# First-pass score chunks of 384 columns dealt out by a table, and GpSimd masking two rows at once and taking over subtractions from VectorE

## The reference

```python
q, k, v = xh @ Wq + bq, xh @ Wk + bk, xh @ Wv + bv       # 8 heads of 16 features
p = pe @ Wp
content = einsum('bqhd,bkhd->bhqk', q + u_bias, k)
pos_score = _rel_shift(einsum('bqhd,khd->bhqk', q + v_bias, p))
score = (content + pos_score) / sqrt(e)
attn = softmax(score, axis=-1)                           # needs each row's maximum
x = x + einsum('bhqk,bkhd->bqhd', attn, v).reshape(b, s, e) @ Wo + bo
# router: x @ Wr1, norm, gelu, @ Wr2, softmax, the two best experts of a token
# each expert: (x @ W1[e])[linear half] * gelu(x @ W1[e])[gate half] @ W2[e]
```

## Time and profile before

| | |
|---|---|
| median of 3 runs | 1703.7 us |
| the profiled execution: its own time | 1698.55 us |
| its span | 1696.8 us |
| busy share of the span | PE 91%, PEld 71%, DVE 83%, ACT 66%, POOL 65% |
| mean granted TensorE clock | 0.948 |

### The profile page before, as it was taken

One profiled execution on the slowest core, in us unless ns is written; L12 is line 12 of the kernel. 1 busy time (PEld: TensorE's weight loads), 2 busy tenths in 40 slices (PEclk: granted clock), 3 DMA queues, 4 the chain that ended last, 5 costly groups with the idle time before them and its releaser, 6 DMA issues. The chain is left out here.

```text
span 1696.8 us, 50747 instructions
## 1 busy us (share of the span) xinstructions
PE 1551.2 (91%) x12534; PEld 1207.3 (71%) x12535; DVE 1402.8 (83%) x5272; ACT 1111.8 (66%) x2303; POOL 1105.3 (65%) x2090
## 2 busy tenths in 40 slices
PE   2599999999999999999999999999952699999997
PEld 1367677777677767777767776777741699999997
DVE  3389889989989988998998998799864588888886
ACT  2127776777777777777777777677730577777775
POOL 3337767776776776777677677567673276666666
PEclk8569999999999999999999999899975799999999
DMA  5624634643653463464355346246453243433433
GB/s 162 192 55 137 184 99 114 182 127 103 170 149 97 137 186 101 112 181 128 103 169 149 97 137 184 71 125 172 127 162 126 43 57 55 57 52 55 57 51 49
DMA packets 131859, 199.97 MB, mean 118 GB/s; under 512 B 18392, under 2 KB 93032, under 8 KB 131648
## 3 DMA queue, kind: packets, MB, share of 16 engines
q1 hardware_dynamic: 105792, 177.20, 36.9%
q0 software_dynamic: 25856, 20.27, 7.9%
HBM read 108.24 MB, written 75.33 MB: 108 GB/s over the span
## 5 line engine op out<-in xcount | busy, mean ns | idle before, releaser
L1063 DVE CUSTOM_DVE_ANT_0 junk<-pA,lmask 128x512 bf16<-128x512 f32 x1056 | 687.1, 683 | 67.6 <-PE pA L651 49.1
L965 ACT ACTIVATE prob<-pB 128x512 f32<-128x512 f32 x384 | 229.8, 599 | 200.9 <-PE pB L670 115.1
L1547 POOL DMA_INDIRECT out<-yb,dst x144 | 231.2, 1605 | 134.7 <-ACT yb L1621 82.7
L672 PE MATMUL pB<-QL,K 97*128 97x512 f32 (+3 forms) x768 | 285.2, 371 | 1.4 <-ACT upper_diag L965 1.2
L649 PE MATMUL pA<-K,QL 96*128 96x512 f32 (+3 forms) x792 | 284.0, 360 | 0.8 <-DVE acc L1069 0.4
L670 PE MATMUL pB<-QU,K 97*128 97x512 f32 (+3 forms) x640 | 266.7, 417 | 0.2
L967 ACT ACTIVATE prob<-pB 128x512 f32<-128x512 f32 x384 | 227.9, 593 | 12.4 <-PE pB L672 4.1
L651 PE MATMUL pA<-K,QU 96*128 96x512 f32 (+3 forms) x660 | 232.8, 354 | 1.6 <-DVE acc L1063 0.3
L688 PE MATMUL pC<-prob,vext 128*17 128x256 f32 x3088 | 217.3, 384 | 0.1
L556 POOL TENSOR_TENSOR prob<-prob,upper_diag 128x128 f32<-128x128 f32 x384 | 179.9, 469 | 31.9
L670 PEld LDWEIGHTS pB<-QU,K 97*128 97x128 f32 x640 | 121.6, 190 | 99.3 <-issue 61.7
(11 more groups left out here) (305 smaller groups left out, 3658.5 us busy)
## 6 DMA issues: line engine op xcount, KB each, us to landing
QL<-split_operands SPq DMA_DIRECT2D x67, 256.0 KB
QU<-split_operands SPq DMA_DIRECT2D x67, 256.0 KB
K<-split_operands SPq DMA_DIRECT2D x67, 256.0 KB
xg<-routed_rows SPq DMA_DIRECT2D x76, 132.0 KB
split_operands<-c_h SPq DMA_DIRECT2D x18, 512.0 KB
split_operands<-c_l SPq DMA_DIRECT2D x18, 512.0 KB
QL<-split_operands SPq DMA_DIRECT2D x67, 128.0 KB
QU<-split_operands SPq DMA_DIRECT2D x67, 128.0 KB
```

Of the source, the lines that this page charges most:

```text
L672: mm = pe.matmul(pB[:, q0 + up:q0 + HALF], K[0:r, s, k], QL[0:r, s, q0 + up:q0 + HALF], start=True, stop=True)
L965: act.activation(p[:, 0:HALF], pB[:, 0:HALF], ACT.Exp, scale=SCALE).then_inc(p_exp, 1)
L1063: v.tensor_tensor_reduce(out, src[:, :], lmask[:, at:at + HALF], 1.0, -3.0e38, ALU.add, ALU.max, acc[:, s, qb, n % 2:n % 2 + 1]).then_inc( ...
L1547: po.indirect_dma_start(dram["out"], bass.IndirectOffsetOnAxis(dst[k][:, a:a + 1], 0), yb[k][:, a, :], None, compute_op=ALU.add).then_inc( ...
```

## The change

**First pass.** It has 24 chunks of 384 columns for each head, three for each block of 128 query rows. The 1152 columns of a query block are now the 1024 keys and its own diagonal block once more: chunk columns up to the diagonal take QL, and those behind it take QU with the keys moved back by 128, so that the diagonal block comes in both forms. One mask `smask` serves all. Columns are as many as before (24 x 384 = 16 x 512 + 8 x 128 = 9216). How many chunks each step gets stands in a table `SHARE` of 8 x 9 numbers between 0 and 5; PE does the first before the second half of the second pass, two more behind it, and what is left behind the context.

**GpSimd.** It masks and adds two rows in one instruction each, at u = 2, 4, 6 and 8, on a view of two `prob` tiles that now lie beside each other. It takes from DVE the six subtractions that read SBUF alone and, at u = 3, `dsup` for the next head. The first batch's low halves stay on DVE. Scatters, position products and residual additions on GpSimd move, most of them to odd steps.

**DVE.** Two low halves (`gu_l`) are left, counted by a semaphore of their own, and `maxima` is one instruction. DVE now waits for `dsup` before it writes new super scores.

```diff
+CHUNK = 3 * P
+SPANS = (S + P) // CHUNK
+S1U = NB * SPANS
-        lmask, umask = sb("lmask", [P, 15 * P], BF16), sb("umask", [P, P])
+        smask = sb("smask", [P, 16 * P], BF16)
-        prob = [keep["b2"]] + [sb(f"prob{i}", [P, S]) for i in range(1, RING)]
+        ring = [keep["b2"], sb("prob23", [P, 2, S])]
+        prob = [ring[i // 2][:, i % 2, :] for i in range(RING)]
-        LOW_AT = {(1, 2): 0, (2, 3): 1, (2, 7): 2, (3, 2): 3, (3, 6): 4, (4, 1): 5, (4, 3): 6, (4, 4): 7}
+        LOW_AT = {(3, 6): 4, (4, 4): 7}
+        SPLIT_AT = {(0, 3): 0, (1, 8): 1, (2, 8): 2, (3, 3): 3, (3, 7): 5, (4, 2): 6}
+        DSUP_AT = 3
...
-        ORDER = (0, 1, 2, 3, 4, 5, 6, 7, 16, 8, 9, 10, 17, 11, 12, 13, 14, 15)
+        SHARE = ((5, 1, 3, 3, 3, 4, 1, 3, 1), (4, 1, 2, 2, 3, 5, 2, 4, 1), (2, 2, 3, 2, 3, 3, 3, 2, 4), (0, 3, 2, 2, 4, 3, 3, 3, 4),
+                 (4, 5, 2, 2, 2, 3, 1, 1, 4), (3, 2, 0, 2, 5, 3, 2, 2, 5), (4, 3, 3, 3, 3, 4, 1, 1, 2), (4, 2, 2, 2, 4, 2, 1, 2, 5))
+        def share(h, u):
+            return range(sum(SHARE[h][:u]), sum(SHARE[h][:u + 1]))
         def piece(n):
-            qb, k0 = n // HPB, (n % HPB) * HALF
-            return qb, k0, min(max(P * (qb + 1) - k0, 0), HALF)
+            qb, c = divmod(n, SPANS)
+            return qb, c, min(max(P * (qb + 1) - CHUNK * c, 0), CHUNK)
# GpSimd
+            def low(nb, n):
+                po.wait_ge(hi_done, have)
+                po.tensor_tensor(parts[name][1][:, cut], src, parts[name][0][:, cut].bitcast(F32), ALU.subtract).then_inc(low_done, 1)
+            def super_difference(b, h):
+                po.wait_ge(mx_done, have)
+                po.tensor_tensor(dsup[:, s, :], acc[:, s, :, 3], mneg[:, s, :].bitcast(F32), ALU.add).then_inc(dsup_done, 1)
...
-                        else:
-                            kb = u - 1
+                        elif u % 2 == 0:
+                            kb = u - 2
+                            p = both_rows.rearrange("p (n q) -> p n q", q=P)[:, kb:kb + NB + 2:NB + 1, :]
                             po.affine_select(out=p, in_=p, compare_op=ALU.is_ge, fill=0.0, base=0,
-                                             pattern=[[1, P]], channel_multiplier=-1).then_inc(lower_masked, 1)
+                                             pattern=[[0, 2], [1, P]], channel_multiplier=-1).then_inc(lower_masked, 1)
-                            po.tensor_tensor(p, p, upper_diag[h % 2][:, P * kb:P * kb + P], ALU.add).then_inc(p_mask, 1)
+                            po.tensor_tensor(p, p, upper_diag[h % 2][:, P * kb:P * kb + 2 * P].rearrange("p (n q) -> p n q", q=P), ALU.add).then_inc(p_mask, 2)
+                        if u == DSUP_AT:
+                            super_difference(b, h + 1)
+                        if (h, u) in SPLIT_AT:
+                            low(b + 1, SPLIT_AT[h, u])
# TensorE, first_pass
+                if low > 0:
+                    mm = pe.matmul(dst[:, 0:low], QL[0:KROWS, s, q], K[0:KROWS, s, k0:k0 + low], start=True, stop=True)
+                if low < CHUNK:
+                    mm = pe.matmul(dst[:, low:CHUNK], QU[0:KROWS, s, q], K[0:KROWS, s, k0 + low - P:k0 + CHUNK - P], start=True, stop=True)
# TensorE, the loop
                         second_pass(b, h, u, 0)
-                        first_pass(b, h + AHEAD, 2 * u)
+                        for n in chunks[:1]:
+                            first_pass(b, h + AHEAD, n)
                         second_pass(b, h, u, 1)
-                        first_pass(b, h + AHEAD, 2 * u + 1)
+                        for n in chunks[1:S1_BUFS]:
+                            first_pass(b, h + AHEAD, n)
                         if u in PAIRS_AT:
                             ...
+                        for n in chunks[S1_BUFS:]:
+                            first_pass(b, h + AHEAD, n)
# VectorE, first_pass
+                v.tensor_tensor_reduce(out, src[:, 0:CHUNK], smask[:, at:at + CHUNK], 1.0, -3.0e38, ALU.add, ALU.max,
+                                       acc[:, s, qb, c:c + 1]).then_inc(s1_read, 1)
# VectorE, maxima
-                v.wait_ge(mx_done, b * H + h + 1)
-                v.tensor_tensor(dsup[:, s, :], acc[:, s, :, 3], mneg[:, s, :].bitcast(F32), ALU.add).then_inc(dsup_done, 1)
```

More of the change, by code:

```diff
@@ L303, in _ @@
                 sp.wait_ge(hi_done, READY[name])
-                sp.wait_ge(low_done, READY[name])
+                if name == "gu":
+                    sp.wait_ge(gu_low, GU_N)
+                else:
+                    sp.wait_ge(low_done, LOWS[name])
                 for op, row in PLACES[name]:
@@ L643, in first_pass @@
                 dst = pA[n % S1_BUFS]
-                n = ORDER[n]
-                if n < NB * HPB:
-                    qb, k0, low = piece(n)
-                    q = slice(P * qb, P * qb + P)
-                    if low > 0:
-                        mm = pe.matmul(dst[:, 0:low], QL[0:KROWS, s, q], K[0:KROWS, s, k0:k0 + low], start=True, stop=True)
-                    if low < HALF:
-                        mm = pe.matmul(dst[:, low:HALF], QU[0:KROWS, s, q], K[0:KROWS, s, k0 + low:k0 + HALF], start=True, stop=True)
-                else:
-                    for i in range(4):
-                        q = slice(P * (4 * (n % 2) + i), P * (4 * (n % 2) + i) + P)
-                        mm = pe.matmul(dst[:, P * i:P * i + P], QU[0:KROWS, s, q], K[0:KROWS, s, q], start=True, stop=True)
+                qb, c, low = piece(n)
+                q, k0 = slice(P * qb, P * qb + P), CHUNK * c
+                if low > 0:
+                    mm = pe.matmul(dst[:, 0:low], QL[0:KROWS, s, q], K[0:KROWS, s, k0:k0 + low], start=True, stop=True)
+                if low < CHUNK:
+                    mm = pe.matmul(dst[:, low:CHUNK], QU[0:KROWS, s, q], K[0:KROWS, s, k0 + low - P:k0 + CHUNK - P], start=True, stop=True)
                 mm.then_inc(s1_ready, 1)
@@ L1047, in low @@
                 v.wait_ge(hi_done, nb * HI_N + n + 1)
-                v.tensor_tensor(parts[name][1][:, cut], src, parts[name][0][:, cut].bitcast(F32), ALU.subtract).then_inc(low_done, 1)
+                v.tensor_tensor(parts[name][1][:, cut], src, parts[name][0][:, cut].bitcast(F32), ALU.subtract).then_inc(gu_low if name == "gu" else low_done, 1)
             def super_out(src, done):
@@ L1058, in first_pass @@
                 src, out = pA[n % S1_BUFS], junk[:, n % S1_BUFS, :]
-                n = ORDER[n]
-                if n < NB * HPB:
-                    qb, k0, _ = piece(n)
-                    at = 7 * P - P * qb + k0
-                    v.tensor_tensor_reduce(out, src[:, :], lmask[:, at:at + HALF], 1.0, -3.0e38, ALU.add, ALU.max,
-                                           acc[:, s, qb, n % 2:n % 2 + 1]).then_inc(s1_read, 1)
-                else:
-                    g = n % 2
-                    for i in range(4):
-                        blk = 4 * g + i
-                        ttr = v.tensor_tensor_reduce(out[:, P * i:P * i + P], src[:, P * i:P * i + P], umask[:, :], 1.0, -3.0e38, ALU.add, ALU.max,
-                                                     acc[:, s, blk, 2:3])
-                    ttr.then_inc(s1_read, 1)
+                qb, c, _ = piece(n)
+                at = 7 * P - P * qb + CHUNK * c
+                v.tensor_tensor_reduce(out, src[:, 0:CHUNK], smask[:, at:at + CHUNK], 1.0, -3.0e38, ALU.add, ALU.max,
+                                       acc[:, s, qb, c:c + 1]).then_inc(s1_read, 1)
             def maxima(b, h):
@@ L1274, in _ @@
             v.tensor_tensor(bo_rows[:, :], bo_rows[:, :], pM[:, 0:E], ALU.add).then_inc(m_done, 1)
-            for n in range(LOW_N):
+            for n in range(HI_N):
                 low(0, n)
@@ L1296, in _ @@
                     for u in range(S2U):
-                        first_pass(b, h + AHEAD, 2 * u)
+                        chunks = share(h, u)
+                        for n in chunks[:1]:
+                            first_pass(b, h + AHEAD, n)
                         for name, place in DVE_OUT.items():
@@ L1300, in _ @@
                                 small_piece(b, name)
-                        first_pass(b, h + AHEAD, 2 * u + 1)
+                        for n in chunks[1:]:
+                            first_pass(b, h + AHEAD, n)
                         if h == 0 and u in NORMALIZE_AT:
@@ L1683, in step @@
                 v.wait_ge(down, i + 1)
-                v.tensor_tensor(yb[k][:, :, :], pY[k % 2][:, :, :], keep["b2"][:, bass.ds(step.experts[k] * E, E)].unsqueeze(1).to_broadcast([P, HALVES, E]), ALU.add).then_inc(y_done, 1)
+                v.tensor_tensor(yb[k][:, :, :], pY[k % 2][:, :, :], keep["b2"][:, 0, bass.ds(step.experts[k] * E, E)].unsqueeze(1).to_broadcast([P, HALVES, E]), ALU.add).then_inc(y_done, 1)
             ex = load_experts(mybir.EngineType.DVE, 0, 2)
```

62 lines of the change are left out of this document (37 added, 25 removed).

## The result

The changed kernel takes 1735.49 us (median of 4 runs, 1732.47 to 1737.46) where the kernel before takes 1702.45 on the same chip (4 runs): 1.0193 times as long, 95% interval 1.0173 to 1.0213, or 33 us more. The forecast was 34 us less. The profiled execution took 1737.46 us, its span is 1735.8.

The account below looks back on a forecast made before the run. The prediction took PE as mostly the engine waited for, with DVE late at a few places and a PE-ACT loop as third limit. Terms -27 - 14 + 7 = -34 us took 1703.7 to 1669.7, say 1670 us; range 1630 to 1706.

Parts of the forecast that it names:

- The table: Chunks per step: steps given less work than the PE-ACT loop's 1.23 us waste the rest, +7 us in all.
- The loop's floor: PE-ACT loop through the single pB buffer: first exponentials stay 1.23 us apart even where PE has less to do.
- the fourth rival: Steps with four or five chunks: bursts starve PE and ACT, 0.5 us each, 38 us slower, 1742 us; chance 0.15.
- First pass on TensorE: First-pass matmuls on PE: without short blocks in a row, 4.74 us a head becomes 4.32, -27 us in all.
- Late VectorE places: Steps (5, 2) and (0, 8), where DVE is late: less work ahead saves 1.8 us a batch, -14 us.
- The two waits: ACT's 1.71 us before `psup` was to shrink, PE's 0.93 us for the router's hidden rows to go.
- First pass on VectorE: DVE's first-pass work: 12.26 us a head both before and after, no change.
- It is hidden: GpSimd's moved work: 3 us less on an engine with 40 us free, so it costs no time.
- The third rival: Port contention: GpSimd's longer instructions hold up DVE, the 14 us for late DVE work are gone, 1684 us; chance 0.05.
- What leaves VectorE: Work taken off DVE: 6.6 us a batch, worth nothing where PE is the one waited for.

Follow-up runs that it names:

- e4: Changed kernel with one even table row, (3, 2, 3, 3, 3, 3, 2, 3, 2) chunks by step, for all eight heads: 1707.5 us, ratio 1.0032.
- e9: e6 with 64 one-column memsets added on VectorE ahead of its batch loop: 1704.2 us, ratio 1.0004 to the kernel before.
- e13: e3 with 64 one-column memsets added on VectorE ahead of its batch loop: 1740.8 us, ratio 1.0253 to the kernel before.
- e12: Changed kernel with its table, TensorE issuing a step's fourth and fifth chunks behind its small pieces and projections: 1716.4 us, ratio 1.0088.
- e15: e9 with a table of at most three chunks a step, fitted twice to steps that lost time: 1684.3 us, ratio 0.9931.
- e5: Changed kernel with only head 0's table row altered, to (2, 2, 3, 3, 3, 4, 2, 3, 2): 1732.5 us, ratio 1.0173.
- e2: Changed kernel with the first pass of the kernel before, so GpSimd's part of the change alone: 1711.2 us, ratio 1.0075.
- e7: e2 with GpSimd's low halves of the loop cut from 512 columns to 8: 1707.9 us, ratio 1.0032.
- e8: Kernel before with six low halves of the loop cut from 512 to 8 columns on VectorE, nothing moved to GpSimd: 1689.3 us, ratio 0.9941.
- e6: Changed kernel with e4's even table, and masks, low halves and sums where the kernel before has them: 1738.1 us, ratio 1.0208.
- e3: Changed kernel with its table, but masks, low halves and differences where the kernel before has them: 1781.1 us, ratio 1.0483.
- e1: Kernel before with only a bounds check on the expert phase's load of its table of additions: 1700.1 us, ratio 1.0002.
- e10: Kernel before with 48 one-column memsets on VectorE ahead of its batch loop: 1701.9 us, ratio 1.0020.

## Why the prediction was wrong, point by point

**The table** is the step that failed. It was priced at +7 us, for steps that get less than the loop's 1.23 us, and its bursts at nothing. It costs 28 us with GpSimd's part (e4) and 37 without (e9 to e13; 42 by the ratios), 18 or 19 of the 28 by what stands behind a burst on TensorE (e12). The loop's floor was right: steps (1, 3), (2, 3), (4, 2) and (5, 2) take 1.24 to 1.27 us with their fewer chunks, as before to 0.01. What I let pass, with "in the steps with bursts DVE has little else, and light steps follow", are the steps with four and five chunks: all 18 are longer than before, by 11.4 us a batch together. The light steps do follow and give back only 6.9 us, so a batch is 4.6 us longer. This is the fourth rival (1742, chance 0.15), with the sign that the prediction names for it, TensorE waiting for VectorE at first-pass chunks. Its 0.5 us a burst is near the mean of 0.64, but the bursts aren't alike: 2.0 us at the loop's way back, up to 4.1 there with the clock, 1.12 at step 5 of head 1, 0.11 at step 4 of head 7. That its 1742 is so near to 1735 is in part luck, since its sum has neither the give-back nor the falls of the clock, and it counts the 34 us of the forecast as gained.

**First pass on TensorE**, -27 us: the mechanism is right, the size is not reached. The starts are the 0.18 us of the forecast. With an even table step 6 of a head falls by 0.27 to 0.34 us in every head (e4). Here is step 6 of head 5 in the kernel before and in e9, by its first exponential and the next step's:

```profile
634.36 0.60 ACT L965 ACTIVATE prob<-pB 128x512 f32<-128x512 f32 x1 [0.49 <-PE pB L670]
636.75 0.60 ACT L965 ACTIVATE prob<-pB 128x512 f32<-128x512 f32 x1 [0.59 <-PE pB L670]
```
```profile
644.34 0.60 ACT L999 ACTIVATE b_all<-pB 128x512 f32<-128x512 f32 x1 [0.58 <-PE pB L697]
646.40 0.60 ACT L999 ACTIVATE prob<-pB 128x512 f32<-128x512 f32 x1 [0.43 <-PE pB L697]
```

2.39 us became 2.06. By the starts of the earlier trace rows this step went from 0.24 + 0.45 to 2 x 0.18 us of first pass, which is just the 0.33; 0.21 of it is the short blocks, and the rest went to other steps with 256 columns. But 18 tiles a head became 24, with the same three to rotate through, and a late VectorE instruction can reach TensorE sooner. That this is why is argued, not shown. e9 gave all of it back (1704), and the best table keeps 1.7 of the 3.4 us a batch (e15: 139.8 against 141.5).

**Late VectorE places**, -14 us: right in the places, not shown in the sum. The two waits went as above, and the steps that held them fell by 1.08 us (head 0, step 8) and 1.18 (head 5, step 3), 2.26 us a batch where 1.8 were forecast. With two chunks instead of one at step 8 of head 0 the gain is gone (e5, +1.13). But what was taken from these steps stands in others: all of head 5 is as long as before to 0.03 us.

**First pass on VectorE**, no change: near enough. A chunk's instructions start 0.48 us apart, 24 of them 11.5 us a head, where 12.26 were forecast.

**GpSimd.** The pair masks take 0.40 + 0.74 us where I had 0.42 + 0.74, the context waits for them once in the whole loop (1.1 us, in its last turn), and GpSimd's busy time fell by 5.8 us a batch. (The sum's lower end is 4 us less, not the 9 that the prediction has.) "It is hidden" was wrong all the same: VectorE's instructions beside GpSimd's are longer (e2). The third rival had the place and 14 us; e2 measured 11 to 13 for this part alone, but the low halves, which the rival priced, are only some of it (e7). In the changed kernel 5 to 10 us of gain are left of it (e13). That the bursts make VectorE the engine that is waited for, so that its relief counts, is a guess.

**What leaves VectorE**, worth nothing where TensorE is waited for: nearly right: two thirds of it gave 1.0 us a batch (e8).

Together: even chunks +4 us (e9, with the memsets), the change's table +37 (e13), GpSimd's part -5. That makes 36 us, where 33 to 35 were measured. These are differences along one path between the two kernels, so that they add up proves nothing; along the path by e2 and e4 GpSimd's part is +11, even chunks -4 and the table +28.

## What to carry to other kernels

When one engine fills a few tiles that a slower one empties, a burst longer than the tiles runs at the emptying engine's pace, and everything queued behind it waits: spread such work evenly, take it away from steps in which the emptying engine is late by the trace, or issue the excess last. A gain by sum over a batch can't be counted on until the order in each step has been checked against the buffers. Work moved to GpSimd was paid here where its instruction stood beside one of VectorE.

## What the runs showed of the hardware

- VectorE can stand still 4.3 to 5.7 us at the end of a loop for nothing that the profile names, each time until 2.2 to 2.5 us after a packet of the instruction queue q14, and 64 one-column memsets ahead of the loop took it away (e6, e9; e3, e13): 34 and 40 us of kernel time. A comparison of two kernels can be off by this much for no reason in their work.
- The granted clock fell to half after TensorE had stood still for VectorE: in e6 in all seven turns of the loop, after 2.7 to 3.6 us, in the changed kernel in two of seven, after 0.99 us, with 0.96 to 1.01 us in the other five too. It also fell with no wait at all: in e4 step 3 of head 6 has eight matmuls of 8 columns in 0.96 us and the clock is low right behind them. The timeline of TensorE there, and the window:

```profile
650.71 0.96 PE L653 MATMUL pE<-hsum,qv 128*128 128x8 f32 x8
...
653.34 1.91 PE L718 MATMUL pC<-b_all,vext 128*17 128x256 f32 x16
```
```profile
652.50:655.50 3.00, 3.00 (x21) 1.48 (x20) 2.29 (x15) 1.25 (x3) 1.89 (x5) 0.52 0.09 28
```

In its profile the kernel before does it in one batch, where steps 4 to 6 of head 6 lose 5.8 us; e1, the same kernel but for the check, in four batches, e4 in seven, e10 in none. A short fall costs 1.4 to 1.6 us. What tips it is open, and it is part of the spread between runs of one kernel.
